# Quantised feed-forward and three attentions: other placing of the up scale, the third weight, the key weights and the first keys

## What is computed

```python
x = x + _L0_xattn_ref(_layernorm(x), ctx, ctx, ...)      # autocorrelation
x = x + _L0_ffn_ref(_layernorm(x), w_gate, w_up, w_down) # quantised feed-forward
x = x + _L1_xattn_ref(...)                               # windowed attention
x = x + _L1_ffn_ref(...)                                 # slot experts, the longest stage
x = x + _L2_xattn_ref(...)                               # full attention
x = x + _L2_ffn_ref(...)
x = x + _L3_xattn_ref(...)                               # attention with rotary embedding
x = x + _L3_ffn_ref(...)

def _L0_ffn_ref(x, w_gate, w_up, w_down):
    def act_qdq(x):                                      # one scale for the whole tensor
        scale = jnp.maximum(jnp.max(jnp.abs(x)) / qmax, 1e-12)
        return jnp.clip(jnp.round(x / scale), -qmax - 1.0, qmax) * scale
    x = act_qdq(x)
    up = act_qdq(x @ lpbq_dequant(w_up).T)
    gate = act_qdq(x @ lpbq_dequant(w_gate).T)
    sig = fixed_qdq_u16(jax.nn.sigmoid(gate))
    gate = act_qdq(gate * sig)
    o = act_qdq(gate * up)
    return o @ lpbq_dequant(w_down).T
# attention: Q = query @ Wq.T + bq, K = key @ Wk.T + bk, V = value @ Wv.T + bv, softmax, output
```

## Time and profile before

| stage | begins at us | lasts us |
|---|---|---|
| autocorrelation | 0 | 124.3 |
| quantised feed-forward | 124.3 | 217.4 |
| windowed attention | 341.7 | 182.1 |
| slot experts | 523.9 | 927.2 |
| full attention | 1451.1 | 167.1 |
| second feed-forward of its kind (receptance) | 1618.2 | 83.6 |
| rotary attention | 1701.9 | 195.8 |
| routed feed-forward | 1897.6 | 344.3 |

### The profile page before, as it was taken

How to read it: one execution, slowest core, us unless ns; L and a number is a source line. 1 busy time by engine, 2 the same in 40 slices (tenths; PEclk the granted TensorE clock), 3 DMA queues, 4 the chain that set the end, 5 groups by cost and what they waited for, 6 DMA issues and landing times. The chain is left out here.

```text
span 2241.9 us, 41356 instructions
## 1 busy us (share of the span) xinstructions
PE 1886.2 (84%) x16363; PEld 1359.0 (61%) x16363; DVE 1496.2 (67%) x3126; ACT 1121.9 (50%) x1939; POOL 159.5 (7%) x123
## 2 busy tenths in 40 slices
PE   7958158895799999999999999789877897599995
PEld 7834045573366666666666666556564465488884
DVE  6677774356767677677777766735566656588886
ACT  3425652445355555555555555334452344267662
POOL 0001300000000000000000000000000000134441
PEclk9969679997899999999999999998998989599998
DMA  4010002002100001000000000010002000457775
GB/s 138 1 44 1 0 1 63 2 2 82 38 20 20 20 21 37 20 20 20 20 20 20 1 1 1 23 41 2 18 0 66 1 2 6 158 194 247 253 243 195
DMA packets 81819, 115.51 MB, mean 52 GB/s; under 512 B 10784, under 2 KB 64224, under 8 KB 81504
## 3 DMA queue, kind: packets, MB, share of 16 engines
q1 hardware_dynamic: 77216, 100.85, 13.8%
q0 software_dynamic: 4416, 12.06, 1.5%
HBM read 102.67 MB, written 10.22 MB: 50 GB/s over the span
## 5 line engine op out<-in xcount | busy, mean ns | idle before, releaser
L2314 PE MATMUL sl_ps_h<-sl_slot_inT,sl_w 128*128 128x512 f16 x1536 | 344.1, 380 | 25.6 <-ACT sl_h L2445 25.5
L2337 PE MATMUL sl_ps_eo<-sl_w,sl_hT 128*128 128x256 f16 x3072 | 353.2, 273 | 0.8 <-DVE sl_hT L2569 0.7
L2337 PEld LDWEIGHTS sl_ps_eo<-sl_w,sl_hT 128*128 128x128 f16 x3072 | 298.5, 98 | 35.9 <-DVE sl_hT L2569 1.3
L2314 PEld LDWEIGHTS sl_ps_h<-sl_slot_inT,sl_w 128*128 128x128 f16 x1536 | 147.9, 98 | 209.3 <-ACT sl_h L2445 41.3
L2569 DVE TENSOR_TENSOR sl_hT<-sl_h,sl_hT 128x512 f16<-128x512 f32 x256 | 177.0, 692 | 86.8 <-ACT sl_hT L2448 82.3
L974 DVE TENSOR_REDUCE at_neg_max<-at_ps 128x8 bf16<-128x1024 f32 x96 | 116.5, 1221 | 162.4 <-PE at_ps L725 162.4
L2445 ACT ACTIVATE sl_h<-sl_ps_h,sl_b1T 128x512 f32<-128x512 f32 x256 | 172.5, 687 | 93.3 <-PE sl_ps_h L2314 86.4
L1885 PE MATMUL mo_ps_h<-mo_xgT,mo_w 128*128 128x256 f16 x1104 | 128.3, 278 | 6.8 <-issue 5.6
L1896 PE MATMUL mo_ps_eo<-mo_w,mo_hT 128*128 128x256 f16 x1104 | 124.1, 273 | 0.0
L1885 PEld LDWEIGHTS mo_ps_h<-mo_xgT,mo_w 128*128 128x128 f16 x1104 | 109.5, 100 | 22.5 <-issue 7.9
L2580 DVE SCALAR_TENSOR_TENSOR sl_result<-sl_ps_eo,sl_b 128x256 f32<-128x256 f32 x128 | 54.3, 425 | 97.9 <-PE sl_ps_eo L2337 93.6
(11 more groups left out here) (370 smaller groups left out, 3704.3 us busy)
## 6 DMA issues: line engine op xcount, KB each, us to landing
mo_w_raw<-in_L_ffn_W SPq DMA_DIRECT2D x46, 1024.0 KB, 7.9
sl_w_in<-in_L_ffn_w SPq DMA_DIRECT2D x16, 1024.0 KB, 5.4
at_ctxT<-ctxT SPq DMA_DIRECT2D x12, 512.0 KB, 7.1
mo_w_raw<-pair_rows SPq DMA_DIRECT2D x4, 1024.0 KB, 9.1
at_wT<-L_attention_w SPq DMA_DIRECT2D x12, 256.0 KB, 6.4
mo_b<-in_L_ffn_b SPq DMA_DIRECT2D x23, 128.0 KB
ac_ctx_all<-in_ctx SPq DMA_DIRECT2D x4, 512.0 KB, 7.7
ac_ctxT<-ctxT SPq DMA_DIRECT2D x4, 512.0 KB, 8.9
```

What stands on the lines that cost most here:

```text
L2314: last = pe.matmul(ps_h[:, j % 2], w1[:, e % 2, w, k, j * P:(j + 1) * P], slot_inT[:, q % 2, x, k].rearrange("p b s -> p (b s)"), start=(k ...
L2337: last = pe.matmul(ps_eo[:, b % 2, 0:D], hT[:, hp, j, b * P:(b + 1) * P], w2[:, e % 2, w, j], start=(j, a) == (0, 0), stop=(j, a) == (HJ - ...
```

## The change

Quantised feed-forward:

- `sig` gets four slots instead of two (`SIG_SLOTS`), two of them in a new tile.
- The up maxima are no longer spread by POOL. PE turns the column of 128 maxima into a row, DVE reduces the row, and PE multiplies the result with a row of ones, which puts it into all partitions (`combine_up_maxima`, `spread_up_maxima`). DVE waits for this at one place, between chunks 3 and 4.
- Evictions and maxima of up follow new tables (`UP_OUT`, `UP_MAXIMA`).
- The third weight is turned in three single tiles, behind the third, fourth and fifth up pair.
- A memset of `ones_row` is added, and the raw third weight lies at another place of `upT`.

Attentions: a new object `Early` holds tiles for the whole program: the identity and two small tables, the turned context of group 0, one set of key weights and the key and query biases. The constants and the context are loaded in the autocorrelation; the key weights and biases of each attention are loaded by SP in the feed-forward ahead of it, behind that stage's own loads. In the windowed and the full attention PE makes the keys of groups 0 and 1 first and stays one group ahead; the rotary one keeps its order. ACT's wait for `bias_made` moves from before the keys to before the queries. The value weights and context groups 1 to 3 are still loaded in the stage itself, earlier in its queue.

The core of the diff:

```diff
@@ autocorrelation, SP
-            load_ctxT(0)
+            env.early.load_constants(sp)
@@ attention, SP
-            load_weight(WK)
-            load_context(0)
-            load_weight(WV)
-            sp.dma_start(bias_cols[:], W["bias"]).then_inc(consts_in, 16)
             for tile, name in consts:
                 sp.dma_start(tile[:], K[name]).then_inc(consts_in, 16)
+            if not rotary:
+                load_context(1)
+            load_weight(WV)
@@ attention, PE
+            pe.wait_ge(early.consts_in, early.CONSTS)
+            pe.wait_ge(early.wk_in, early.key_weights_in(layer))
+            if not rotary:
+                for o in range(C):
+                    project_keys(0, o)
             for g in range(G4):
-                for o in range(C):
-                    project_keys(g, o)
-                if g == 0:
+                if rotary or g + 1 < G4:
+                    for o in range(C):
+                        project_keys(g if rotary else g + 1, o)
+                if rotary and g == 0:
                     pe.wait_ge(consts_in, CONSTS)
@@ attention, ACT
-            act.wait_ge(consts_in, CONSTS)
-            act.wait_ge(bias_made, 1)
+            act.wait_ge(early.consts_in, early.CONSTS)
+            act.wait_ge(early.wk_in, early.key_weights_in(layer))
@@ quantised_ffn, tables
-EVICTED_BY_GATE = (((0,), (1,)), ((2,), (3,)), ((4, 5), (6,)), ((7, 8), (9, 10)), ((11,), ()), ((), ()))
-MAXIMA_BY_GATE = (((4,), (5, 6)), ((7,), (8, 9)), ((10,), (11,)), ((), ()), ((), ()), ((), ()))
+UP_OUT = (((0,), (1,)), ((2,), (3,)), ((4, 5), ()), ((6, 7), ()), ((8, 9), ()), ((10, 11), ()))
+UP_MAXIMA = ((2, 3), (4, 5), (6, 7), (8, 9, 10, 11), (), ())
+SIG_SLOTS = 4
@@ quantised_ffn, POOL
             for c in range(FC):
                 round_sigmoid(c)
-                if c == 3:
-                    combine_maxima(US)
@@ quantised_ffn, PE
+            def combine_up_maxima():
+                pe.wait_ge(max_made, US + 1)
+                pe.transpose(ps_out[0:1, 0, 0:P], own_max[:, US:US + 1], ident[:]).then_inc(up_max_turned, 1)
+                pe.wait_ge(up_max_made, 1)
+                pe.wait_ge(made_consts, 4)
+                pe.matmul(ps_out[:, 1, 0:1], ones_row[0:1], up_max[0:1], start=True, stop=True).then_inc(max_all, 1)
@@
-                if q == PAIRS_EACH:
-                    turn_weights(2)
+                if PAIRS_EACH + 2 <= q <= PAIRS_EACH + 4:
+                    turn_weights_tile(q - PAIRS_EACH + 4)
             pe.wait_ge(w_ready, 9)
+            combine_up_maxima()
@@ quantised_ffn, ACT
             for c in range(FC):
                 round_gate(c)
-                if c == 0:
-                    weights_high(2)
-                for q in EVICTED_BY_GATE[c][0]:
+                for q in UP_OUT[c][0]:
                     evict(UP, PAIRS_EACH + q)
+                if c == 1:
+                    weights_high_tile(7)
                 sigmoid(c)
-                for q in EVICTED_BY_GATE[c][1]:
+                for q in UP_OUT[c][1]:
                     evict(UP, PAIRS_EACH + q)
+                if c in (0, 1):
+                    weights_high_tile((6, 8)[c])
@@ quantised_ffn, DVE
-            weights_low(2)
-            for q in range(4):
+            for q in range(2):
                 max_hidden(UP, PAIRS_EACH + q)
             for c in range(FC):
+                if c == 0:
+                    weights_low_tile(6)
                 silu(c)
+                if c in (0, 1):
+                    weights_low_tile(7 + c)
+                max_silu(c)
+                for q in UP_MAXIMA[c]:
                     max_hidden(UP, PAIRS_EACH + q)
-                if c == 2:
+                if c == 3:
                     begin_scale(US, PAIRS_EACH, hidden_max, 2 * PAIRS_EACH)
-                if c == 3:
+                    spread_up_maxima()
                     finish_scale(US)
```

More of the change, by code:

```diff
@@ L1331, in pair, with sig @@
             return ps[:, 2 * (q % 3):2 * (q % 3) + 2]
+        def sig(c):
+            slot = c % SIG_SLOTS
+            return xT[:, slot] if slot < C else sig_more[:, slot - C]
         def pair_at(q):
@@ L1459, in sigmoid @@
                 act.wait_ge(gate_rounded, c + 1)
[L1460 to L1461 removed]
+                enough(act, silu_made, c + 1 - SIG_SLOTS)
+                act.activation(sig(c), low_half(gateT[:, c]), ACT.Sigmoid, scale=scale[:, GS:GS + 1]).then_inc(sig_made, 1)
             def round_up(c):
```

169 lines of the change are left out of this document (104 added, 65 removed).

## The result

The changed kernel took 2212.6 us in the median of four runs (2208.8 to 2220.5), against 2245.2 of the kernel before (four runs, 2242.7 to 2245.5): ratio 0.986, 95% interval 0.983 to 0.989, 32.6 us less. Measured again beside the later experiments, on another occasion, it took 2212.3 us (five runs, 2209.2 to 2216.6), ratio 0.987 (0.985 to 0.989). The forecast was 2217.0. The execution whose profile stands here is the slowest of the first four: 2220.5 us, span 2218.6. A second profile, from the later measurement ("after, second profile"), has a span of 2212.5. One run of the kernel before, among those beside the third group of experiments, took 3232.3 us at a mean granted clock of 0.58; it is left out of every median and ratio.

A forecast was written before the change was run, and what follows sets the result against it. Bounds taken: DVE's chain with one hole in the quantised feed-forward, waits at the attentions' heads. 12.8 - 0.2 + 6.0 + 5.1 + 3.4 = 27.1 us off 2243.67 gives 2216.6, stated as 2217.0; range 2211 to 2220, chance 0.62.

The forecast's parts named there:

- Quantised stage, 12.8 less 0.2: Feed-forward: silu scale begins at 252.3 to 252.6 instead of 265.26, gaining 12.8 us, less 0.2 allowed for the memset.
- The spread: Feed-forward: DVE waits 2.0 us for PE to spread the up maxima, between bounds of 0.48 and about 3.0.
- just in time: Feed-forward: POOL, needing 6.8 us after the gate's all-reduce, is ready at 204.9 for the sigmoid ending at 205.1.
- POOL's margins: Feed-forward: POOL finishes chunks shortly before DVE asks; two margins below 1.3 us, silu collisions costing 3.5 us at most.
- Autocorrelation, slot experts, receptance at 0: Stages predicted to gain 0; autocorrelation's two added small transfers cost at most 1 us.
- Windowed attention, 6.0: Head of windowed attention: keys 1 end at 351.1, 6.0 us gained, 3.0 less if the clock falls in the short gap.
- Full attention, 5.1: Head of full attention: keys 0 end at 1457.9, keys 1 at 1461.5; 5.1 us gained, range 2.0 to 6.5.
- Rotary attention, 3.4: Head of rotary attention: DVE's waits for constants (1.81) and for PE's swap (1.61) vanish, 3.4 us gained.
- A: Attention heads bound by late landings and low clock, each gaining just 3.4 us: 2221 us, chance 0.17.
- B: Feed-forward: POOL needs longer after the gate's all-reduce or meets the silus, stage gains 6: 2223 us, chance 0.11.
- C: Feed-forward: PE's clock sinks between up pairs, 5.2 us a pair instead of 2.6, stage gain gone: 2229 us, chance 0.05.
- D: Slower: clock sinks longer, from the first up pair and 10 us after the pause in each attention: 2266 us, chance 0.02.

The follow-up runs named there:

- third group of experiments: Four of the twelve follow-up kernels, sharing a chip and runs of the kernel before, whose median there was 2245.6 us.
- both kernels' score loops filled: Kernel before and changed kernel, each with unread matmuls in PE's gaps at the start of its score loops: 2230.5 us and 2196.6 us.
- the kernel with the feed-forward's part alone: Kernel before with only the quantised feed-forward changed, the attentions' loads and key order kept: 2226.8 us, ratio 0.992.

## Why the prediction was right, and where its steps were off

- **Quantised stage, 12.8 less 0.2.** Measured 13.1 and 13.7 us over the stage, 13.7 with both kernels' score loops filled. The first silu was put at 209.2 and came at 209.39; the silu scale at 252.3 to 252.6 and came at 253.13, of which 1.7 is the one collision, whose price had been given as up to 1.73. The spread was taken as 2.0 and took 1.5. POOL "just in time" held: it began its first clamp at 205.48, right behind the sigmoid. The prediction had two slips here. By its own numbers three of POOL's margins are below 1.3 us (0.4, 0.3 and 1.2), not two, so the collisions could have cost 5.2, not 3.5; one silu was held. And it took a silu's maximum as 2.2 where its rows step by 2.32, which makes 27.8 of its 27.1 (in the run the step is 2.2 where an up maximum follows, so little came of it). The four slots do not "make this order possible": with two, the third sigmoid doesn't wait either. The 0.2 for the memset is shown by no run.
- **Autocorrelation, slot experts, receptance at 0.** The first two within 1.2 us (slot experts 1.1 less in the first profile, nothing in the second). Receptance was 2.1 to 2.5 us longer in both profiles, with 21 us low in place of 10; it was 85.9 us with 21 low also in the kernel that adds no transfer to it, so the added transfer isn't the cause.
- **Windowed attention, 6.0.** The step was right where it was made: 6.3 and 6.6 us at the first scores. Of these some 2.2 were the clock in the head of the kernel before: with both filled the heads are 56.3 and 52.0, a gain of 4.3; the head of before had 7 us low in it there and 10 without the filling, which touches no head, and took 57.3 with 7 low in the kernel with the feed-forward's part alone. The mis-sized term is therefore this one, by up to 1.7. Inside the head, the first keys were put at 3.5 us and took 5.37 in the first profile and 3.67 in the second, and the second group's keys started 5.4 and 5.0 us after the stage's start, where 5.8 was forecast. What the prediction left out is the start of the score loop. It looked for a sinking clock in the head and in the up pairs, and took the loop behind as moving as one; in the profiled execution that loop ran 24 us at half clock, which cost 5.2 us more than before and left 1.1 of the gain.
- **Full attention, 5.1.** 6.1 and 5.4; 5.6 with both filled. The first keys took 5.28 and 6.00 us in place of 6.62.
- **Rotary attention, 3.4.** 4.5 and 4.0 over the stage; 4.5 and 3.9 at the first scores; 3.0 with both filled (2.7 at the first scores). Both DVE waits are gone.
- **The total.** 27.1 was worked out. The sum has a slip: the profiled execution was put 1.6 us below the median, which makes 2218.2, but only 0.4 were added. The first profile gives 23.3 in its span, the second 29.4, the medians 32.6 and 29.2. The median of the first measurement is 4.4 us below the forecast: the quantised stage gave 1 more, full and rotary attention together up to 2, and what is left is within what the same stages show from one execution to the next. With the score loops filled the four stages give 13.7 + 4.3 + 5.6 + 3.0 = 26.6, close to 27.1; that it is so close is partly luck, since the terms missed by 1.1, -1.7, 0.5 and -0.4.
- **The rivals.** A fell: the heads gained 3.9 to 6.6 us each. But its wait was not gone: in the second profile PE stands still 1.09 us for the second context group in windowed attention; in the first, the slower first keys covered it. B's collision came once, at its price, and its long switch after the gate's all-reduce didn't. C fell: the up pairs ran at full clock. Its argument against, that rows at 76% busy have the clock at 1.00, is no safe sign: the router's rows are busy for 19.18 of 20 us at 0.50. The Trainium skill ("TensorE: Matmul & The Clock Gate", section "A second HAM failure mode: psum-queue depth-cycling") would have small pauses between groups of matmuls swing the clock; between up pairs, with pauses of 0.2 to 1.0 us, the trace doesn't show it; at the start of the score loops, with pauses of 1 to 2.5, the clock falls, once, and for 3 to 24 us. D named the right mechanism at the wrong place: not at the projections behind the first pause, but at the first scores, and for 24 us in one attention rather than 30 in three; full and rotary attention have 17 to 21 us low there in both kernels, so the change lost nothing by it.

## What to carry to other kernels

Look at the granted clock not only where a change makes or removes a wait, but at the next place where PE starts a serial chain: a stage that is moved forward can pay its gain back there, and one profile can't say how often. Where several executions of a kernel differ by 10 us, compare variants with the clock held by matmuls that nobody reads, measured to be shorter than the gap that they fill; here that took the low level out of every score loop, made the kernel 15.7 us faster, and showed what the change's own stages are worth. An engine that changes between two kinds of work at 6 us a time should do all of the one kind first, and the change that is left must be hidden too: on the path it cost 3.4 to 4.0 us.

## What the runs showed of the hardware that was not expected

- PE can be busy for 19.2 of 20 us and stay at the lower granted level, at which it was when the rows began (it had idled 7.21 us before them): the router's transposes and 8-column matmuls ran so at 1.17 us a row. One 128-column f32 matmul more per row, after five of 256 columns in front, and the same rows ran at full clock at 0.84 us.
- At the low level the score loop lost about a third of the time that it spent there, not half. The two profiles of after show why: at the low level the 32 score matmuls take 2.09 us in place of 1.17, but PE's waits for DVE and ACT are as long at either level (2.54 low and 2.56 full, 0.99 and 1.02, 1.45 and 1.44).
- POOL pays 5.99 us in front of an all-reduce and 6.80 behind it, and the 5.99 begin when it arrives there, whether or not the instruction's input is ready (1.5 us before the maxima were).
- When DVE's silu with two SBUF inputs and POOL's clamp want to start together, either may be held for most of the other's time (3.99 in place of 2.28 on DVE, or 4.06 in place of 1.90 on POOL), and which it is differs between executions of the same kernel.
